# Weights turned by transposing DMAs, and a new order of the last three attention batches

## The chip, the cores and the metric

The kernel runs on one core of one Trainium2 chip. The time is device microseconds of that core for one execution; the figure given is the median of 3 runs.

## The reference

A gated block of two layers over `x` of 8 batches x 256 positions x 256 channels, all in float32. The first is single-head attention with a context of the same shape (the softmax runs over the queries of each key, axis 1), the second a gated feed-forward layer with 704 hidden units, whose inputs and weights are rounded to integers of 8 bits with a scale (per row for weights, one scale of the whole tensor for activations).

```python
def attention(q, c, Wq, Wk, Wv):
    qh, kh, vh = q @ Wq.T, c @ Wk.T, c @ Wv.T
    s = qh @ kh.T / sqrt(256)
    s = where(causal, s, -inf)
    return softmax(s, axis=1) @ vh

def ffn(x, clip_x, clip_down, w_gate, w_up, w_down):
    xq = fake_quant(x, clip_x)               # one scale: sigmoid(clip) * max|x| / 127
    gate, up = xq @ q8(w_gate).T, xq @ q8(w_up).T
    h = fake_quant(silu(gate) * up, clip_down)
    return h @ q8(w_down).T

x = x + tanh(g_xattn) * attention(layernorm(x), ctx, Wq, Wk, Wv)
x = x + tanh(g_ffn) * ffn(layernorm(x), ...)
```

The two maxima over the whole tensor (of the normalised input, and of the hidden values) are barriers: nothing behind one can start before everything ahead of it is done.

## The kernel before

All is held in SBUF. Every engine runs a program written by hand, and semaphores join them; nothing but that written order sets what an engine does next. PE is TensorE, DVE VectorE, ACT ScalarE, POOL GpSimd, SP the engine that issues most transfers.

Stage one, attention, goes over 8 batches (LAST is 7). For batch b PE makes `scores(b)` (L497), the projected queries of the next batch, `project_queries(b + 1)` (L479), the values of the batch after that, `values(b + 2)` (L457), and the weighted sum `attend(b)` (L507 to L509). DVE takes the row maxima (`row_max`, L941), ACT the exponentials (L744, L749), DVE the inverse sums, and scales the queries of the next batch by their row's inverse deviation (`scale_queries_whole`, L933, into `uT`); ACT scales the values (`values_out`, L759, into `vh`). `scores(b + 1)` waits for that `uT`. The deviations come for batches 4 to 7 by two small transfers on SP's queue (`spread`, then `r_wide`). After `attend(b)` DVE adds the residual (L955), takes the statistics for the second layer norm (L961, L967), POOL normalises (L388, into `xn2`), and DVE takes the largest absolute value (`largest2`, L972). Of the last batch the residual is made in PSUM by PE (L598 to L608), one tile in bank RB and one in SC, and DVE takes its statistics there (L1074, L1076).

The weights of the second layer are rounded meanwhile: gate and up by ACT (`quantise_weights`, the last step L773, into `wgu_q`, 6 slots of 128 rows), down by ACT and POOL (`quantise_down_weights` L778, and L404, into `wd_q`). PE needs them turned, with the contracted index on the partitions. PE turns gate and up with 24 transposes in three groups of 8 (`turn_gate_up`, L527), one group between `attend(5)` and `scores(6)` and two between `project_queries(7)` and `scores(7)`; ACT (L783, twice) and DVE (L1058) copy the results from PSUM. The down weights are turned at the end of stage two (`turn_down`, L537) and copied by ACT (L788 to L796).

The first barrier: DVE's maxima of the last two batches (L1079), then their largest (L1083), a spreading matmul on PE (L544), the scale and its inverse (L1089, L1092), then the rounded input `xq`. Stage two makes gate and up (L650) for five blocks of 128 hidden units in two halves, and a block of 64 (L669). The second barrier is the maximum of the hidden values (L1129), again through L544, L1089 and L1092. Ahead of it PE turns the residual stream (L680), which ACT copies to `x1T` (L801): six of eight copies ahead of the barrier, two behind. Stage three goes over 8 steps of 256 rows (c = 0 to 7): ACT rounds (L890), DVE clips to `hq` (L1164), PE multiplies by the down weights (L705, L710), DVE adds the residual (`finish`, L1169), SP stores.

## Time and profile before

| what | value |
|---|---|
| median of 3 runs | 109.54 us (109.43 to 109.54) |
| the profiled execution | 109.32 us, of which the trace's span is 107.4 us |
| granted clock of TensorE | full (1.00) all through |
| busy: PE, DVE, ACT, POOL | 93%, 76%, 65%, 41% of the span |
| chain that ended last, by engine | PE 52%, ACT 18%, DVE 17%, issue 4%, DMA 4% |

The chain that ended last is followed back from the last instruction, at each step to what released it. A share of it says where time was spent with nothing beside it to hide it; a busy share says only how much an engine worked.

### The profile page before, as it was taken

What the parts mean: (1) busy time and instruction counts of PE and PEld (TensorE: products, weight loads), DVE (VectorE), ACT (ScalarE), POOL (GpSimd) and SP (SyncE); (2) the same over time, 40 slices, a digit from 0 to 9 for tenths busy, and PEclk for the clock granted to TensorE, in tenths of its full rate; (3) what the DMA queues carried; (4) which work ended last, traced back from release to release, by engine and by line L of the source; (5) the groups of instructions that cost most, each with busy time, mean ns of one, the idle gap of its engine ahead of it and who ended that gap; (6) DMA issues with size and microseconds to landing.
All of it is one profiled execution on the core that took longest, in us unless ns stands there. A gap on an engine that the chain in (4) does not pass through costs nothing.

```text
span 107.4 us, 1812 instructions
## 1 busy us (share of the span) xinstructions
PE 99.9 (93%) x600; PEld 76.8 (71%) x600; DVE 81.6 (76%) x212; ACT 69.6 (65%) x131; POOL 44.2 (41%) x80
## 2 busy tenths in 40 slices
PE   5989999999999999999999987999999699999960
PEld 2268888988989897988988973444433398788850
DVE  0275296597899979868678978649999997869990
ACT  0422252567882817457677978889988899999800
POOL 7215035065371817343192593065578540520000
PEclk9999999999999999999999999999999999999999
DMA  3999999999001411305000000000000000005547
GB/s 28 383 384 260 386 419 422 410 406 395 31 23 26 33 16 14 38 1 57 0 0 0 0 0 0 6 0 3 0 0 0 0 6 0 0 0 195 195 148 249
DMA packets 5769, 12.18 MB, mean 113 GB/s; under 512 B 1280, under 2 KB 2048, under 8 KB 5760
## 3 DMA queue, kind: packets, MB, share of 16 engines
q1 hardware_dynamic: 5184, 11.28, 31.8%
q10 hardware_dynamic: 576, 0.79, 2.1%
q8 instruction: 5, 0.08, 0.3%
q14 instruction: 4, 0.03, 0.1%
HBM read 9.96 MB, written 2.10 MB: 112 GB/s over the span
## 4 chain that ended last, share of the span: by engine, by line
PE 52%; ACT 18%; DVE 17%; issue 4%; DMA 4%; ACTq 1%; DVEq 0%
PE ps L457 13%; PE ps L479 11%; PE ps L497 10%; ACT ints L890 7%; DVE shared L1124 5%; DVE hmax L1129 4%; ACT xn L801 4%; DMA wq_sb<-in_wq 4%; PE ps L650 3%; PE ps L507 3%; PE ps L509 2%; PE ps L508 2%; PE ps L554 2%; ACT silu L863 2%; PE ps L669 2%
## 5 line engine op out<-in xcount | busy, mean ns | idle before, releaser
L650 PE MATMUL ps<-xq,wguT 128*128 128x512 bf16 x80 | 17.7, 379 | 0.8 <-DVE xq L1104 0.8
L428 POOL TENSOR_TENSOR shared<-up_sb,silu 128x1024 f32<-128x1024 f32 x5 | 11.8, 2365 | 9.7 <-ACT up_sb L868 9.7
L650 PEld LDWEIGHTS ps<-xq,wguT 128*128 128x128 bf16 x80 | 7.6, 98 | 10.6 <-DVE shared L1124 1.1
L457 PE MATMUL ps<-wvT,shared 128*128 128x256 f32 x56 | 13.3, 380 | 0.0
L479 PE MATMUL ps<-shared,a_sb 128*128 128x256 f32 x56 | 13.2, 379 | 0.0
L1129 DVE TENSOR_REDUCE hmax<-shared 128x1 f32<-128x2048 f32 (+1 forms) x6 | 12.7, 2108 | 0.6
L863 ACT ACTIVATE silu<-ps,gu_scale 128x1024 f32<-128x1024 f32 x10 | 11.1, 1115 | 2.5 <-PE ps L650 2.5
L744 ACT ACTIVATE probs<-neg_scores,neg_max 128x256 f32<-128x256 f32 x8 | 4.1, 508 | 12.7 <-DVE neg_max L941 12.5
L497 PE MATMUL ps<-uT,shared 128*128 128x256 f32 (+1 forms) x64 | 11.9, 329 | 0.0
L457 PEld LDWEIGHTS ps<-wvT,shared 128*128 128x128 f32 x56 | 10.6, 190 | 1.6 <-issue 0.2
L497 PEld LDWEIGHTS ps<-uT,shared 128*128 128x128 f32 x64 | 10.7, 190 | 1.2
L705 PE MATMUL ps<-hq,wdT 128*128 128x256 bf16 x80 | 10.9, 274 | 0.3 <-DVE hq L1164 0.2
L479 PEld LDWEIGHTS ps<-shared,a_sb 128*128 128x128 f32 x56 | 10.1, 190 | 1.1
L375 POOL TENSOR_SCALAR var<-mv 128x2 f32<-128x2 f32 x8 | 1.5, 193 | 21.9 <-DVE mv L967 21.7
L890 ACT ACTIVATE ints<-shared,act_inv 128x1408 int16<-128x1408 f32 (+2 forms) x9 | 9.5, 1128 | 0.0
L759 ACT ACTIVATE vh<-ps,inv_sum 128x256 f32<-128x256 f32 x16 | 6.7, 471 | 2.8 <-DVE inv_sum L950 2.8
L1124 DVE SCALAR_TENSOR_TENSOR shared<-ps,gu_scale,silu 128x1024 f32<-128x1024 f32 x5 | 6.4, 1279 | 2.7 <-ACT silu L863 2.7
L955 DVE SCALAR_TENSOR_TENSOR xs<-ps,tanh_g,xs 128x512 f32<-128x512 f32 x7 | 5.2, 747 | 3.7 <-PE ps L509 3.7
L705 PEld LDWEIGHTS ps<-hq,wdT 128*128 128x128 bf16 x80 | 6.8, 98 | 1.5 <-DVE hq L1164 0.6
L941 DVE CUSTOM_DVE_ANT_0 neg_scores<-ps,causal 128x256 f32<-128x256 f32 (+1 forms) x16 | 5.0, 350 | 2.6 <-PE ps L497 2.6
L388 POOL TENSOR_SCALAR xn<-xs,neg_mean,rstd 128x256 f32<-128x256 f32 x12 | 6.6, 557 | 0.8 <-POOL neg_mean L383 0.2
L1169 DVE SCALAR_TENSOR_TENSOR xn<-ps,out_scale,xn 128x256 f32<-128x256 f32 x16 | 6.8, 475 | 0.0
(131 smaller groups left out, 200.0 us busy)
## 6 DMA issues: line engine op xcount, KB each, us to landing
shared<-in_xc SPq DMA_DIRECT2D x6, 512.0 KB, 10.6
out<-xn SPq DMA_DIRECT2D x7, 256.0 KB, 2.0
xs<-in_x SPq DMA_DIRECT2D x3, 512.0 KB, 8.3
shared<-in_wgu SPq DMA_DIRECT2D x3, 512.0 KB, 7.7
shared<-in_xc SPq DMA_DIRECT2D x4, 256.0 KB, 6.0
wd<-in_wd SPq DMA_DIRECT2D x1, 768.0 KB, 10.2
r_wide<-spread SPq DMA_DIRECT2D x4, 128.0 KB, 4.0
wq_sb<-in_wq ACTq DMA_DIRECT2D x1, 256.0 KB, 3.9
```

What stands on the lines that cost most here:

```text
L428: nc.gpsimd.tensor_tensor(hid[:, 2 * i + 1, :], up_sb[i % 2][:], silu1[i % 2][:], ALU.mult).then_inc(hid_done[1], 1)
L457: last = nc.tensor.matmul(bank2(VB[b])[:, k, :], ctxT(b)[:, e, k * P:(k + 1) * P], weights[:, e, :], start=(e == 0), stop=(e == KT - 1))
L479: last = nc.tensor.matmul(query_bank(b, f), a_sb[:, e, f * P:(f + 1) * P], xT(b)[:, e, :], start=(e == 0), stop=(e == KT - 1))
L497: last = nc.tensor.matmul(bank(SC)[:, c0:c0 + n], ctxT(b)[:, f, k * P:(k + 1) * P], uT[b % 2][:, f, k * P:S], start=(f == 0), stop=(f == K ...
L650: last = nc.tensor.matmul(bank(4 * half + 2 * g + c), wguT[:, i, g, k, :], xq[:, k, col:col + CH], start=(k == 0), stop=(k == KT - 1))
L705: nc.tensor.matmul(down_half(c, t), wdT[:, i, cols], hq[c % HQ_BUFS][:, 2 * i:2 * i + 2, :].rearrange("p h n -> p (h n)"), start=(i == 0), ...
L759: last = nc.scalar.activation(vh[b % 2][:, k, :], bank2(VB[b])[:, k, :], ACT.Copy, scale=inv_sum[:, b, k:k + 1])
L863: nc.scalar.activation(dst[:], ps[:, 4 * half:4 * half + 2, :].rearrange("p c n -> p (c n)"), ACT.Silu, scale=gu_scale[:, i, 0:1]).then_in ...
L890: nc.scalar.activation(hq_i16[c % HQ_BUFS][:, s0:s1, :], hid[:, s0:s1, c * P:(c + 1) * P], ACT.Copy, scale=act_inv[:, 1:2]).then_inc(hq_in ...
L1124: nc.vector.scalar_tensor_tensor(out=hid[:, 2 * i, :], in0=ps[:, 2:4, :].rearrange("p c n -> p (c n)"), scalar=gu_scale[:, i, 1:2], in1=si ...
L1129: nc.vector.tensor_reduce(hmax[:, n:n + 1], hid[:, first:first + count, :].rearrange("p s n -> p (s n)"), AX.X, ALU.max, apply_absolute_va ...
L1169: return nc.vector.scalar_tensor_tensor(out=x1T[:, c, t, :], in0=down_half(c, t), scalar=out_scale[:, t:t + 1], in1=x1T[:, c, t, :], op0=A ...
```

## The change

Three things are changed. (1) Gate, up and down weights are turned by transposing DMAs on SP's queue, from SBUF to SBUF (2 bytes an element): six of 128 x 512 for gate and up, two of 128 x 896 for down, issued behind the last `r_wide`. The transposes on PE and the copies out of PSUM go away. The down weights are laid out in 7 blocks of 128 in place of 6 (the half block stands twice, beside zeros), so its load, its rounding and its cast are 896 columns wide in place of 768. POOL's cast to `wd_q` comes ahead of the second normalisation of batch 5. (2) In the last three batches `scores(6)` and `scores(7)` come ahead of `attend(5)` and `attend(6)` in turn; half of `values(7)` is made behind them; DVE's maxima `largest2(3)` to `largest2(5)` move. (3) All eight copies to `x1T` stand ahead of the second barrier.

```diff
@@ SP
+            for s in range(SLOTS):
+                sp.wait_ge(wgu_q_done, s + 1)
+                sp.dma_start_transpose(wguT[:, s].rearrange("p n k i -> p (n k) i"),
+                                       wgu_q[:, s].rearrange("p n d -> p (n d)")).then_inc(wguT_here, 16)
+            sp.wait_ge(wd_q_done, 1)
+            for t in range(KT):
+                sp.dma_start_transpose(wdT[:, :, t * P:(t + 1) * P], wd_q[:, t]).then_inc(wdT_here, 16)
@@ POOL
+                if b == LAST - 1:
+                    pool.wait_ge(wdint_done, KT)
+                    nc.gpsimd.tensor_copy(wd_q[:], wd_i16[:]).then_inc(wd_q_done, 1)
                 if 1 <= b < LAST:
                     inverse_deviation2(b - 1)
                     apply2(b - 1)
-                if b == LAST - 1:
-                    pool.wait_ge(wdint_done, KT)
-                    nc.gpsimd.tensor_copy(wd_q[:], wd_i16[:]).then_inc(wd_q_done, 1)
@@ PE
-                values(b + 2)
+                if b + 2 < LAST:
+                    values(b + 2)
+                else:
...
+                    values_tile(LAST, 0)
                 if b + 2 < WIDE_FROM:
                     spread_deviation(b + 2)
-                attend(b)
+                if b < LAST - 2:
+                    attend(b)
 
             p = LAST % 2
-            pe.wait_ge(vh_ready, LAST - 1)
-            turn_gate_up(0, WT)
             scores(LAST - 1)
             project_queries(LAST)
-            pe.wait_ge(wguT_ready, 1)
-            turn_gate_up(1, WT)
-            turn_gate_up(2, X2)
+            attend(LAST - 2)
             scores(LAST)
             attend(LAST - 1)
-            pe.wait_ge(wguT_ready, 2)
-            transposes2(LAST - 2)
+            values_tile(LAST, 1).then_inc(v_done, 1)
...
-            for b in (0, 1, 2):
+            for b in (0, 1, 2, 4, 5):
                 transposes2(b)
-            pe.wait_ge(wguT_last, 1)
-            transposes2(4)
...
-            pe.wait_ge(wguT_ready, 2)
-            pe.wait_ge(wguT_last, 1)
+            pe.wait_ge(wguT_here, 16 * SLOTS)
...
-            pe.wait_ge(silu_done[1], FULL)
-            turn_down(0, 4)
-            turn_down(1, 5)
...
+            pe.wait_ge(wdT_here, 16 * KT)
@@ ACT
-            wguT_out(0, WT)
             exponentials(LAST - 1)
             values_out(LAST - 1)
-            wguT_out(1, WT)
...
-            wdT_out()
-            for c in range(STEPS - 2):
+            for c in range(STEPS):
                 x1T_out(c)
...
-            for c in (STEPS - 2, STEPS - 1):
-                x1T_out(c)
@@ DVE
+            row_max(LAST - 1)
+            largest2(LAST - 4)
+            invert_sum(LAST - 1)
+            scale_queries_whole(LAST)
+            largest2(LAST - 3)
+            residual(LAST - 2)
+            stats2(LAST - 2)
             row_max(LAST)
-            largest2(LAST - 2)
+            variance2(LAST - 2)
             for k in range(QT):
...
             residual(LAST - 1)
             stats2(LAST - 1)
             variance2(LAST - 1)
+            largest2(LAST - 2)
```

On PE, from the values of the last batch (the `wvT_g` rows) to the last scores (`uT1` the second time): `vh1` belongs to batch 5, `uT0` to batch 6. Before:

```order
L457 MATMUL ps<-wvT_g,shared 128x256 x4
L507 MATMUL ps<-vh1,probs0_1 128x256
L508 MATMUL ps<-vh1,probs0_1 128x256
L509 MATMUL ps<-vh1,probs1_1 128x256
L527 MATMUL ps<-ident_bf,wgu_q 128x128 x8
L497 MATMUL ps<-uT0,shared 128x256 x2
L497 MATMUL ps<-uT0,shared 128x128 x2
L479 MATMUL ps<-shared,a_sb 128x256 x4
L527 MATMUL ps<-ident_bf,wgu_q 128x128 x16
L497 MATMUL ps<-uT1,shared 128x256 x2
L497 MATMUL ps<-uT1,shared 128x128 x2
```

In the changed program, to the weighted sum of batch 6 (`vh0`), whose last two rows and the other half of the values follow:

```order
L460 MATMUL ps<-wvT_g,shared 128x256 x2
L498 MATMUL ps<-uT0,shared 128x256 x2
L498 MATMUL ps<-uT0,shared 128x128 x2
L480 MATMUL ps<-shared,a_sb 128x256 x4
L508 MATMUL ps<-vh1,probs0_1 128x256
L509 MATMUL ps<-vh1,probs0_1 128x256
L510 MATMUL ps<-vh1,probs1_1 128x256
L498 MATMUL ps<-uT1,shared 128x256 x2
L498 MATMUL ps<-uT1,shared 128x128 x2
L508 MATMUL ps<-vh0,probs0_0 128x256
```

The rows L527 are gone, two of the four value products have left the stretch, and the weighted sum of batch 5 stands behind the scores of batch 6 and the queries of batch 7.

On DVE, from the scaled queries of batch 7 (`uT1`, the last `r_wide` row) to the maxima of the last batch in PSUM. Before:

```order
L933 TENSOR_TENSOR uT1<-ps,r_wide 128x512
L1058 COPY wguT<-ps 128x1024
L972 TENSOR_REDUCE xmax<-xn2 128x1
L941 ISA neg_scores1,neg_max<-ps,causal 128x256
L941 ISA neg_max 128x1
L941 ISA neg_scores1,neg_max<-ps,causal 128x128
L941 ISA neg_max 128x1
L972 TENSOR_REDUCE xmax<-xn2 128x1
L1067 RECIPROCAL inv_sum<-row_sum 128x1 x2
L955 SCALAR_TENSOR_TENSOR xs<-ps,tanh_g,xs 128x512
L961 BN_STATS bn2<-xs 128x6 x2
L967 BN_AGGR mv2<-bn2 128x2 x2
```

In the changed program:

```order
L887 TENSOR_TENSOR uT1<-ps,r_wide 128x512
L926 TENSOR_REDUCE xmax<-xn2 128x1
L909 SCALAR_TENSOR_TENSOR xs<-ps,tanh_g,xs 128x512
L915 BN_STATS bn2<-xs 128x6 x2
L895 ISA neg_scores1,neg_max<-ps,causal 128x256
L895 ISA neg_max 128x1
L895 ISA neg_scores1,neg_max<-ps,causal 128x128
L895 ISA neg_max 128x1
L921 BN_AGGR mv2<-bn2 128x2 x2
L1023 RECIPROCAL inv_sum<-row_sum 128x1 x2
L909 SCALAR_TENSOR_TENSOR xs<-ps,tanh_g,xs 128x512
L915 BN_STATS bn2<-xs 128x6 x2
```

The copy L1058 is gone, the residual and the statistics of batch 5 now stand between the queries of batch 7 and the last row maxima, and `largest2(5)` (the second xmax row before) has left its place behind the last row maxima. It now stands behind the statistics of batch 6, ahead of those of batch 7, where the changed program goes on:

```order
L921 BN_AGGR mv2<-bn2 128x2 x2
L926 TENSOR_REDUCE xmax<-xn2 128x1
L1031 BN_STATS bn2<-ps 128x6
L1033 BN_AGGR mv2<-bn2 128x2
L1031 BN_STATS bn2<-ps 128x6
```

So the one maximum, which had the wait for the exponentials to fill, now has a place in the row of work that ends in the barrier's maximum.

On SP's queue, from the last two small transfers of the deviations to the stores, in the changed program:

```order
L330 DMA spread<-rstd1 128x2
L333 DMA r_wide<-spread 128x256
L337 DMA_TRANSPOSE wguT<-wgu_q 128x4x128 x6
L341 DMA_TRANSPOSE wdT<-wd_q 128x7x128 x2
L345 DMA out_0<-xn2 128x512 x7
L348 DMA out_0<-xn2 128x256 x2
```

The eight transposing transfers stand between the last `r_wide` and the first store; before, the stores followed at once.

## Rows read from the trace of the kernel before

**Rows 1.** Chain of waits, last three batches: start us, length us, what.

```profile
44.41 1.31 PE ps L497 x8
45.72 1.73 PE ps L479 x8
47.45 1.73 PE ps L457 x8
49.17 0.43 PE ps L507 x2
...
50.47 0.45 PE ps L527 x8
...
54.01 0.89 PE ps L527 x16
...
56.48 0.42 DVE neg_scores L941
...
58.13 0.66 DVE xs L955
...
61.02 1.29 DVE xmax L1079 x4
...
65.61 2.77 PE ps L650 x12
```

**Rows 2.** Timeline of DVE: start us, length us, engine line op.

```profile
44.45 0.75 DVE L955 SCALAR_TENSOR_TENSOR xs<-ps,tanh_g,xs 128x512 f32<-128x512 f32 x1 [0.23 <-PE ps L509]
45.23 0.75 DVE L961 BATCH_NORM_STATS2 bn<-xs 128x6 f32<-128x256 f32 x2
45.90 0.41 DVE L941 CUSTOM_DVE_ANT_0 neg_scores<-ps,causal 128x256 f32<-128x256 f32 x1
...
47.69 0.69 DVE L933 TENSOR_TENSOR uT<-ps,r_wide 128x512 f32<-128x512 f32 x1
...
57.04 0.68 DVE L972 TENSOR_REDUCE xmax<-xn 128x1 f32<-128x512 f32 x1
```

**Rows 3.** Timeline of ACT, same columns.

```profile
48.58 1.75 ACT L778 ACTIVATE wd_i<-wd,wdinv 128x768 int16<-128x768 f32 x2
...
57.89 0.84 ACT L759 ACTIVATE vh<-ps,inv_sum 128x256 f32<-128x256 f32 x2
...
60.94 0.82 ACT L841 ACTIVATE neg_dev<-ps,mv 128x256 f32<-128x256 f32 x2
```

**Rows 4.** Timeline of POOL, same columns.

```profile
53.21 0.19 POOL L375 TENSOR_SCALAR var<-mv 128x2 f32<-128x2 f32 x1 [3.83 <-DVE mv L967]
...
55.62 1.46 POOL L404 CAST wd_q<-wd_i 128x1536 bf16<-128x1536 int16 x1
```

**Rows 5.** Timeline of SP's queue, same columns.

```profile
46.88 0.32 SPq L337 DMA_DIRECT2D r_wide<-spread  x1
```

**Rows 6.** DMA issues on the page: KB each, median us to landing.

```profile
out<-xn SPq DMA_DIRECT2D x7, 256.0 KB, 2.0
...
r_wide<-spread SPq DMA_DIRECT2D x4, 128.0 KB, 4.0
```

**Rows 7.** Instructions of tile wgu_q: ns min/median/max, first and last start.

```profile
L773 ACT CAST wgu_q<-wgu_i x6: 617/618/619, 19.7 to 43.6; 128x512 bf16<-128x512 int16 x6
```

**Rows 8.** Chain of waits, after the last hidden block.

```profile
88.53 3.03 ACT xn L801 x6
...
94.47 0.95 ACT xn L801 x2
```

**Rows 9.** Timeline of DVE in the last stage.

```profile
91.48 0.87 DVE L1160 TENSOR_SCALAR ints<-shared,act_inv 128x384 int16<-128x384 f32 x2
...
96.39 0.53 DVE L1164 TENSOR_SCALAR hq<-ints 128x1408 bf16<-128x1408 int16 x1 [0.49 <-ACT ints L890]
96.84 0.87 DVE L1169 SCALAR_TENSOR_TENSOR xn<-ps,out_scale,xn 128x256 f32<-128x256 f32 x2
...
101.83 0.53 DVE L1164 TENSOR_SCALAR hq<-ints 128x1408 bf16<-128x1408 int16 x1
```

More of the change, by code:

```diff
@@ L34 @@
 SLOTS = FULL + 1
+WD_BLOCKS = FULL + 2
 STEPS = NT // 2
@@ L518, in transposes2 @@
                 last.then_inc(tr2_done, 1)
-            def turn_gate_up(n, bk):
-                pe.wait_ge(wgu_q_done, 2 * n + 2)
-                view = ps[:, bk, :].bitcast(BF16).rearrange("p (s n k i) -> p s n k i", s=2, n=2, k=KT)
-                for s in range(2):
-                    for g in range(2):
-                        for k in range(KT):
-                            last = nc.tensor.transpose(view[:, s, g, k, :],
-                                                       wgu_q[:, 2 * n + s, g, k * P:(k + 1) * P], ident_bf[:])
-                last.then_inc(wgu_tr, 1)
-            def turn_down(n, bk):
-                pe.wait_ge(wd_q_done, 1)
-                view = ps[:, bk, :].bitcast(BF16)[:, 0:3 * D].rearrange("p (s h) -> p s h", s=3)
-                for s in range(3):
-                    i0 = (3 * n + s) * P
-                    for t in range(KT):
-                        last = nc.tensor.transpose(view[:, s, t * P:(t + 1) * P], wd_q[:, t, i0:i0 + P], ident_bf[:])
-                last.then_inc(wd_tr, 1)
             def spread_max(n, bk):
@@ L682, in turn_x1 @@
                 last.then_inc(x1_turned, 1)
[L684 removed]
+            pe.wait_ge(silu_done[1], FULL)
             turn_x1(0)
             turn_x1(1)
[L687 removed]
+            pe.wait_ge(up_out_done, FULL)
             turn_x1(2)
             turn_x1(3)
[L690 removed]
+            pe.wait_ge(silu_done[0], FULL + 2)
             turn_x1(4)
             turn_x1(5)
[L693 removed]
+            pe.wait_ge(hid_done[0], FULL + 2)
             turn_x1(6)
             turn_x1(7)
[L696 removed]
+            pe.wait_ge(x1T_ready, 4)
             spread_max(1, 7)
@@ L710, in down_products @@
                             last = nc.tensor.matmul(down_half(c, t)[:, half * P:(half + 1) * P],
-                                                    wdT_rest[:, half, cols], hq[c % HQ_BUFS][:, 2 * FULL, :],
+                                                    wdT[:, FULL + half, cols], hq[c % HQ_BUFS][:, 2 * FULL, :],
                                                     start=False, stop=(half == 1))
                         last.then_inc(down_done, 1)
+            pe.wait_ge(wdT_here, 16 * KT)
             first = FIRST_SLOTS // 2
@@ L779, in quantise_down_weights @@
                     wdint_done, 1)
-            def wguT_out(n, bk):
-                act.wait_ge(wgu_tr, n + 1)
-                nc.scalar.copy(wguT[:, 2 * n:2 * n + 2].rearrange("p s n k i -> p (s n k i)"),
-                               ps[:, bk, :].bitcast(BF16)).then_inc(wguT_ready, 1)
-            def wdT_out():
-                act.wait_ge(wd_tr, 1)
-                nc.scalar.copy(wdT[:, 0:3, :].rearrange("p s h -> p (s h)"),
-                               ps[:, 4, :].bitcast(BF16)[:, 0:3 * D]).then_inc(wdT_ready, 1)
-                act.wait_ge(wd_tr, 2)
-                nc.scalar.copy(wdT[:, 3:5, :].rearrange("p s h -> p (s h)"),
-                               ps[:, 5, :].bitcast(BF16)[:, 0:2 * D]).then_inc(wdT_ready, 1)
-                act.wait_ge(rest_zeroed, 1)
-                for half in range(2):
-                    rows = slice(half * REST, (half + 1) * REST)
-                    nc.scalar.copy(wdT_rest[rows, half, :],
-                                   ps[rows, 5, :].bitcast(BF16)[:, 2 * D:3 * D]).then_inc(wdT_ready, 1)
             def x1T_out(c):
@@ L1027, in _ @@
             dve.wait_ge(consts, 3)
-            for b in range(LAST):
+            for b in range(LAST - 1):
                 if b >= 1:
@@ L1225 @@
     down = given["L0_ffn_w_down"].reshape(KT, P, I).transpose(1, 0, 2)
+    none = np.zeros((P, KT, P - REST), np.float32)
     scalars = np.concatenate([given[name].reshape(1) for name in
@@ L1235 @@
         "wgu": np.stack([slots(given["L0_ffn_w_gate"]), slots(given["L0_ffn_w_up"])], axis=2),
-        "wd": np.concatenate([down, down[:, :, FULL * P:I]], axis=2),
+        "wd": np.concatenate([down, none, none, down[:, :, FULL * P:I]], axis=2),
     }
```

45 lines of the change are left out of this document (15 added, 30 removed).

## The prediction

> **What bounds the kernel now.** I read first the page (granted clock, shares by engine, the chain by line), then the chain of waits in order of time over the last three attention batches, then the timelines of DVE, ACT, POOL and SP's queue beside it, and the chain again behind the last hidden block. The clock is full all through, so nothing hangs on it. Up to the last scores the chain is PE alone, piece behind piece: scores 1.31 us, queries 1.73, values 1.73, the three parts of a weighted sum 0.43 each [rows 1]. What PE does there ahead of the last scores is paid for in full, the turning of the gate and up weights too: 0.45 us ahead of the scores of batch 6, 0.89 ahead of those of batch 7 [rows 1]. At 56.48 DVE takes over with the last row maxima, and but for the exponentials the chain stays on DVE through the residual of batch 6 (58.13) and the four maxima (61.02) up to the barrier; PE starts stage two at 65.61 [rows 1]. Behind the second barrier ACT leads: its copies to x1T run from 88.53 to 91.56, and two more hold it for 0.95 us at 94.47 [rows 8].
>
> **The change, part by part.**
>
> *PE up to the last scores.* Same work up to the queries of batch 6, which end at 47.45 [rows 1]. Then half of the values (0.86) leads to 48.31. The scores of batch 6 wait for their scaled queries, which DVE has at 47.69 + 0.69 = 48.38 [rows 2]: call it 48.40, a new wait of 0.1. Behind the waiting PE instruction stands everything that follows, so its end counts. Then scores 1.31, queries 1.73, weighted sum of batch 5 1.30, scores of batch 7 1.31: 54.05 [rows 1], with a tail of 0.16 of the last product about 54.2, an estimate from the 45.90 at which DVE follows a product piece that ends at 45.72 [rows 1, 2].
>
> Does the second scaling hold this up? From the row maxima of batch 5 (45.90) to the end of the scaling that follows (48.38) is 2.48 [rows 2]. Those of batch 6 start at 49.9 (48.40 + 1.31 and the tail), so the scaling ends at 52.4, ahead of the 52.74 at which PE comes to the last scores. ACT must be free for the exponentials in between, 0.7 behind the row maxima, at 50.6. Its two roundings of the down weights run from 48.58 for 1.75 [rows 3]; with 896 columns for 768 I add 0.2 (a sixth of 1.75 would be 0.3, an upper bound), which gives 50.5. It just fits. The two copies of turned weights on ACT and the one on DVE go; they lay beside other work, so they are worth nothing by themselves.
>
> *DVE from there to the barrier.* DVE ends the scaling at 52.4 (the next piece can start at 52.3), takes a maximum of an already normalised batch (0.60, by 0.68 less its overlap [rows 2]) and starts the residual of batch 5 at 52.93, when PE's weighted sum is there too. From a residual to the row maxima behind it is 45.90 - 44.45 = 1.45 [rows 2], so the last row maxima start at 54.38, 0.2 behind what PE alone would allow. Before it was 56.48 [rows 1]: 2.10 us earlier. From here DVE's row is the same as before, with one piece more on it: the maximum of batch 5, which before stood at 57.04 in the hole that the exponentials leave [rows 2], now stands behind the statistics of batch 6, at 0.60. So the barrier comes 2.10 - 0.60 = 1.50 us earlier.
>
> Three others must follow. POOL normalises batch 5 from 53.21 to 55.62 [rows 4], 2.4 us behind the variance; that now comes at about 55.2, so the input of the moved maximum is there at 57.7, and DVE comes to it at 54.38 + 3.37 = 57.75 (3.37 is what lay between 56.48 and the end of the variance of batch 6, 1.7 behind 58.13 [rows 1]). That is a margin of nothing, and each tenth by which POOL is later counts. The cast of the down weights, 1.46 at 55.62 [rows 4], 1.7 with 1792 columns, goes first on POOL, from 50.5 to 52.3, so it holds up nothing, and frees POOL behind. ACT: values_out of the last batch started at 57.89 [rows 3]; it now waits for the other half of the values, 54.05 + 1.30 + 0.86 + tail = 56.4, also 1.5 earlier, so its deviations, done at 60.94 + 0.82 = 61.76 before [rows 3], are there at 60.3, and DVE's fourth maximum starts at 60.5. PE has the transposes of batches 4 and 5 behind the last products; five batches, each about a piece of 0.43 [rows 1], end at 60.6, before the spreading matmul is due at 61.3.
>
> *The transposing DMAs.* The trace has none. The last weights are rounded at 43.6 + 0.6 = 44.2 [rows 7], but SP issues the last r_wide at 46.88 for 0.32 [rows 5], and the transposes stand behind it: from 47.2. PE needs all six at 65.61 - 1.50 = 64.1. So six transfers of 128 KB have 16.9 us, 2.8 each if they don't overlap at all. Below, the cost is nothing (they overlap, and beside them the DMA engines have nothing but r_wide). Above, the slowest transfer of 128 KB in this trace, r_wide with 4.0 us to landing, six times in a row [rows 6]: 24 us, to 71.2, 7.1 late. The stores move 256 KB in 2.0 us [rows 6]; six in a row would end at 59.2. I take the lower end, hidden: contiguous rows of 1 KB read from SBUF are nearer to a store than to a broadcast of one row of HBM, and queued transfers overlap. The two down transposes can follow from 52.3 and have until 91 even at 4.0 each. SP's stores come behind them at 95, so its queue is free.
>
> The Trainium skill has a rule that speaks against this. "VectorE: DVE Perf Modes", section "The three transpose paths", puts one 128 x 128 block of 2 bytes at 1309 ns by DMA and 390 ns on TensorE; here a group of 8 blocks took PE 0.45 us, 56 ns each in the row [rows 1], so the page's figure for TensorE does not hold for blocks in a row. If the page's DMA figure held in a row for 24 blocks, it would be 31.4 us, to 78.6, 14.5 us late, and the time some 122 us; no run yet shows it.
>
> *Loads.* The down weights' load is 896 KB for 768, and the cover is that its first reader, and those of the loads behind it, come microseconds after the last load. Nothing counted.
>
> *Behind the second barrier.* ACT's eight copies to x1T, 3.03 / 6 = 0.51 each, take 4.0 us from about 86.7 and end before the barrier. ACT then starts rounding with DVE, at 91.48 in place of 91.56 [rows 8, 9]: 0.08. The 0.95 of copies leaves ACT's row [rows 8]. But the pitch of stage three was (101.83 - 96.39) / 4 = 1.36, and DVE alone needs 0.45 for a clip (96.84 - 96.39) and 0.87 for two finishes [rows 9], 1.32 and small gaps. So little of the 0.95 comes through: over some five steps 0 to 0.2. With the 0.08 I take 0.15 in all; bounds 0 and 0.95 + 0.08.
>
> **Sum.** 109.32 - 1.50 - 0.15 = 107.67 for a profiled execution; the median of the runs is 0.22 above the profiled one, so 107.9.
>
> **The rivals.**
> 1. *The transposes are late* (slower). PE's first gate product waits for the sixth. It costs nothing up to 16.9 us for the six and decides the sign at 18.5 us, 3.1 each in a row. With 4.0 each: 109.54 - 1.65 + 7.1 = 115.0. For it: a 2-byte transpose writes pieces much smaller than a store's; against it: 17 us with idle DMA engines. 0.15. The rule above is this case at its worst.
> 2. *The transposes push back the last r_wide* (slower). DVE now wants it at 49.9 + (47.69 - 45.90) = 51.7 [rows 2]; it lands at about 46.88 + 4.0 = 50.9 [rows 5, 6], a margin of 0.8. Its data shares the DMA engines with transposes issued right behind it. If landing takes 8.0 for 4.0, the scaling starts 3.2 late, and the time is 107.9 + 3.2 = 111.1; the sign turns at 2.4 us of delay. Against it: it was issued first on the same queue. 0.06.
> 3. *The front gives less.* DVE has almost no slack in the new order: the late normalisation by POOL, ACT's rounding, the residual ahead of the row maxima each can add some tenths. Gain 0.3 to 1.1, time 108.4 to 109.2. 0.12.
> 4. *Nothing comes of it*: 109.3 to 109.8, if two of those meet. 0.05.
> The forecast has 0.62, with a range of its own of 107.4 to 108.4 (front 1.1 to 1.7, end 0 to 0.5).
>
> **How the numbers follow.** 0.2% is 0.22 us, about what a measurement of this kernel can tell. Faster: 0.62 + 0.12 = 0.74; same 0.05; slower 0.15 + 0.06 = 0.21. The range reaches from 107.3 (a bit more of the 0.95 comes through) over rivals 3 and 4 to 109.8, and leaves out the two slower cases.
>
> **What would show it.** In the changed profile: scores of batch 6 near 48.4 with a wait of about 0.1 for the scaling; the last row maxima at 54.4; the first maximum over the deviations at 59.5; the first gate product at 64.1, released by DVE's xq. If it is released by a DMA, rival 1; if the scaling of batch 7 waits for a DMA, rival 2; if largest2(5) waits for POOL, rival 3. Landing times of the transposes: under 2.8 each in a row. Stage three's pitch 1.33 to 1.36, released by DVE or PE and no more by ACT. What would make it wrong is above all a transposing DMA of several microseconds.

## The result, and the profile after

The changed kernel takes **106.86 us** (median of 4 runs, 106.51 to 106.93) beside 109.54 of the kernel before on the same chip: ratio 0.9749, 95% interval 0.9726 to 0.9772, 2.7 us less. The forecast was 107.9 us with a range from 107.3 to 109.8. The sign came as said, by the front part that was named, but the time lies below the range. The comparison was made twice more, on other occasions, each time with its own runs of before: 0.9805 (0.9773 to 0.9838) and 0.9822 (0.9789 to 0.9856), 2.0 to 2.1 us less. So the gain is 2.0 to 2.7 us, and why it varies is a question of its own below. A ratio leaves out executions in a slower state of the chip, which shows as a lower granted clock or as a time over 1.5% above the kernel's fastest.

The page of the changed kernel: span, busy time by engine, the granted clock and DMA rows in 40 slices, and the chain by engine.

```profile
span 104.7 us, 1734 instructions
PE 97.4 (93%) x562; PEld 75.0 (72%) x564; DVE 80.7 (77%) x211; ACT 66.1 (63%) x125; POOL 43.9 (42%) x79
PEclk9999999999999999999999999999999999999999
DMA  3999999999323010402946500000000000005555
DMA packets 10888, 13.54 MB, mean 129 GB/s; under 512 B 6400, under 2 KB 7168, under 8 KB 10880
PE 56%; DVE 28%; ACT 6%; issue 4%; POOL 3%; DVEq 0%; POOLq 0%
```

ACT's share of the chain fell from 18% to 6%, and the page's summary of the chain lists no DMA. The transposes are the 9465 in the middle of the DMA row (50 to 60 us); no engine waits for them. The chain of waits from batch 6 to the first gate product, against [rows 1]:

```profile
48.35 1.59 PE ps L498 x8
...
56.08 0.66 DVE xs L909
...
59.58 1.29 DVE xmax L1036 x4
```

The timeline of DVE in the same stretch (start us, length us), against [rows 2]:

```profile
47.61 0.69 DVE L887 TENSOR_TENSOR uT<-ps,r_wide 128x512 f32<-128x512 f32 x1
...
51.77 0.69 DVE L887 TENSOR_TENSOR uT<-ps,r_wide 128x512 f32<-128x512 f32 x1
...
54.45 0.41 DVE L895 CUSTOM_DVE_ANT_0 neg_scores<-ps,causal 128x256 f32<-128x256 f32 x1
...
57.81 0.69 DVE L926 TENSOR_REDUCE xmax<-xn 128x1 f32<-128x512 f32 x1
```

Then those of ACT, POOL and SP's queue, against [rows 3 to 5]:

```profile
48.49 1.97 ACT L755 ACTIVATE wd_i<-wd,wdinv 128x896 int16<-128x896 f32 x2
```

```profile
50.52 1.68 POOL L404 CAST wd_q<-wd_i 128x1792 bf16<-128x1792 int16 x1 [1.38 <-ACT wd_i L755]
```

```profile
47.22 0.32 SPq L333 DMA_DIRECT2D r_wide<-spread  x1
47.58 7.82 SPq L337 DMA_TRANSPOSE wguT<-wgu_q  x6
55.45 2.64 SPq L341 DMA_TRANSPOSE wdT<-wd_q  x2
```

The last row maxima start at 54.45 and not at 56.48, the first maximum over the deviations at 59.58 and not at 61.02 in the chain. Six transposes are issued in 7.82 us, one each 1.30; in the third comparison's profile the six took 9.95. On the page their landing stands beside that of the loads and stores, against [rows 6]:

```profile
out<-xn SPq DMA_DIRECT2D x7, 256.0 KB, 2.0
...
r_wide<-spread SPq DMA_DIRECT2D x4, 128.0 KB, 3.9
...
wguT<-wgu_q SPq DMA_TRANSPOSE x6, 2.5
wdT<-wd_q SPq DMA_TRANSPOSE x2, 3.0
```

The last of the six is issued at 54.1 and is there at about 56.6, 7.5 us before the first gate product is due (the page has 78 of the 80 gate and up records of L630, so the first shown, at 64.38, may not be the first made). In the last stage, ACT and then DVE, against [rows 8, 9]:

```profile
89.71 9.36 ACT L846 ACTIVATE ints<-shared,act_inv 128x384 int16<-128x384 f32 x9 [0.75 <-DVE act_inv L1049]
```

```profile
92.79 0.56 DVE L1121 TENSOR_SCALAR hq<-ints 128x1408 bf16<-128x1408 int16 x1 [0.37 <-ACT ints L846]
...
94.05 0.51 DVE L1121 TENSOR_SCALAR hq<-ints 128x1408 bf16<-128x1408 int16 x1
...
95.27 0.51 DVE L1121 TENSOR_SCALAR hq<-ints 128x1408 bf16<-128x1408 int16 x1
...
99.11 0.53 DVE L1121 TENSOR_SCALAR hq<-ints 128x1408 bf16<-128x1408 int16 x1
...
100.58 1.80 DVE L1126 SCALAR_TENSOR_TENSOR xn<-ps,out_scale,xn 128x256 f32<-128x256 f32 x4 [0.17 <-PE ps L686]
```

Two more lines of before belong beside these, a clip ahead of those in [rows 9] and the finishes at the end:

```profile
94.56 0.57 DVE L1164 TENSOR_SCALAR hq<-ints 128x1408 bf16<-128x1408 int16 x1 [0.36 <-ACT ints L890]
...
102.27 2.44 DVE L1169 SCALAR_TENSOR_TENSOR xn<-ps,out_scale,xn 128x256 f32<-128x256 f32 x6
```

Before, the clips stood 1.83 us apart once (94.56 to 96.39, with ACT's two copies in between), then four times 1.36, 7.27 in all. Changed, the same five distances are 1.26, twice 1.22, 1.26 and at last 1.36 again, 6.32 in all (92.79 to 99.11). The last clip comes 0.95 us earlier, the whole length of the two copies. ACT itself still needs 1.36 for a step of 1408 columns, as two more lines of its timeline show (starts of pieces), and PE, on which the chain stays to the end, 0.66 for half a step:

```profile
94.90 2.81 ACT L846 ACTIVATE ints<-shared,act_inv 128x1408 int16<-128x1408 f32 x2
96.26 2.81 ACT L846 ACTIVATE ints<-shared,act_inv 128x1408 int16<-128x1408 f32 x2
```

```profile
96.60 0.55 PE ps L681 x5
97.14 0.11 PE ps L686 x2
97.25 0.55 PE ps L681 x5
```

With the two spans cut at four marks, the 2.7 us fall into pieces (the spans are printed to 0.1 us, so the last piece is no more exact):

| stretch | before | after | difference |
|---|---|---|---|
| start to the first stage-two rounding on DVE (63.85, 62.41) | 63.85 | 62.41 | -1.44 |
| from there to the last stage's first rounding (91.48, 89.71) | 27.63 | 27.30 | -0.33 |
| from there to the end of DVE's last finish (104.71, 102.38) | 13.23 | 12.67 | -0.56 |
| from there to the end of the span | 2.7 | 2.3 | -0.4 |

The experiments ask what makes each of these, and what makes the runs of the changed kernel differ. Unless said otherwise each starts from the changed kernel. A ratio is to the kernel before, run beside the variant; its median was 109.5 to 109.6 each time.

### The profile page after: what moved, and what is told of

It is laid out like the page before. It is cut to its first block, busy times and chain, and to the rows that moved or that the text cites. A ratio compares the mean times of both kernels' runs of the same rounds, so it can differ in the third digit from the quotient of the medians.

```text
span 104.7 us, 1734 instructions
## 1 busy us (share of the span) xinstructions
PE 97.4 (93%) x562; PEld 75.0 (72%) x564; DVE 80.7 (77%) x211; ACT 66.1 (63%) x125; POOL 43.9 (42%) x79
## 3 DMA queue, kind: packets, MB, share of 16 engines
q1 hardware_dynamic: 10304, 12.66, 37.8%
## 4 chain that ended last, share of the span: by engine, by line
PE 56%; DVE 28%; ACT 6%; issue 4%; POOL 3%; DVEq 0%; POOLq 0%
PE ps L460 12%; DVE hmax L1086 9%; PE ps L681 9%; PE ps L480 8%; PE ps L498 8%; PE ps L450 4%; DVE shared L1081 4%; PE ps L630 2%; POOL shared L431 2%; PE ps L508 2%; DVE bn L915 2%; PE ps L510 2%; PE ps L509 2%; DVE xs L909 2%; PE ps L535 2%
## 5 line engine op out<-in xcount | busy, mean ns | idle before, releaser
L630 PE MATMUL ps<-xq,wguT 128*128 128x512 bf16 x78 | 17.2, 379 | 1.1 <-DVE xq L1061 1.0
L630 PEld LDWEIGHTS ps<-xq,wguT 128*128 128x128 bf16 x80 | 7.8, 98 | 10.2 <-issue 1.0
```

The source lines that it names most:

```text
L630: last = nc.tensor.matmul(bank(4 * half + 2 * g + c), wguT[:, i, g, k, :], xq[:, k, col:col + CH], start=(k == 0), stop=(k == KT - 1))
```

## Experiments

**The last stage: ACT's two late copies.** First they go back behind the barrier, with all else as changed:

```
-            for c in range(STEPS):
+            for c in range(STEPS - 2):
                 x1T_out(c)
...
             hidden_ints(2, 0, THIRD_ACT_SLOTS)
+            for c in (STEPS - 2, STEPS - 1):
+                x1T_out(c)
```

> The changed kernel with the last two copies to x1T back behind the second barrier, where the kernel before had them: 0.95 us more on ACT ahead of its rounding of step 3. The prediction's theory (DVE's own pitch of 1.32 us bounds stage three, so the copies are worth 0.1 or so): 107.0 us. The theory from the trace after (ACT's late rounding made DVE do its last six finishing pieces in one burst behind the last clip, and the last three stores in one burst behind them): all that stage three and its tail gained, up to 0.9 us, comes back: 107.6 to 107.8 us, with DVE's last piece again some 0.9 us behind PE's last product in place of 0.6.

Beside it the changed kernel itself:

> The changed kernel itself, as a base for the others of this call. 106.9 us (106.7 to 107.1). The open question is the gap of 0.4 us on DVE ahead of the second product of stage two, there in the trace of the kernel before and not in that of the changed one: if it belongs to the program, it is absent here too; if it comes and goes, it may be here.

Measured: 108.40 us (0.9888, interval 0.9853 to 0.9923) against 107.41 (0.9805). By the ratios that is 0.9 us, with 0.5 of uncertainty. DVE's timeline with the copies back:

```profile
94.85 0.53 DVE L1123 TENSOR_SCALAR hq<-ints 128x1408 bf16<-128x1408 int16 x1 [0.49 <-ACT ints L846]
...
100.73 2.44 DVE L1128 SCALAR_TENSOR_TENSOR xn<-ps,out_scale,xn 128x256 f32<-128x256 f32 x6
```

This is the picture of before: the clip waits for ACT, and six finishes are left for one burst at the end. From DVE's first rounding to its last finish it takes 13.23 us, to the hundredth what before took, and the tail 2.5 for 2.3. So in the trace the copies cost 0.56 + 0.2, about 0.7 to 0.8 us.

Then the same question asked of the kernel before (the waits for eight copies are lowered to six as well):

```
-            for c in (STEPS - 2, STEPS - 1):
-                x1T_out(c)
```

> The kernel before, with ScalarE's two copies of the last two blocks of the transposed stage-two input left out (the last steps then read stale columns there, and the output of those is another). Everything else is as before. Theory 'the two copies set the pitch of stage three': ScalarE's integers and with them VectorE's clips come 0.95 us earlier, VectorE's last six finishing pieces spread out, the last stores too: 0.6 to 0.95 us less than the kernel before, so 108.6 to 108.9 us. Rival (the prediction's own reading, TensorE's 1.32 us a step bounds): 0.15 to 0.3 us less, 109.2 to 109.4. Its VectorE instructions are those of before up to the end of stage two: if the 0.41 us ahead of product(1) belong to the kernel before, they are here again.

0.9955 (0.9926 to 0.9985), 0.5 us less, between the two theories. Its profiled execution ran with a granted clock of 0.853 throughout (span 131.1 us), so its rows don't price the copies. It was made again, with the pause of the next paragraph out of the way:

> The kernel before with the four small VectorE instructions at its start (109.11 us measured) and with ScalarE's two late copies left out (the last two blocks of the transposed stage-two input stay stale, and the output of the last steps is another). Theory 'the two copies set the pitch of stage three': 0.6 to 0.9 us less than 109.11, so 108.2 to 108.5 us, and in the profile VectorE's finishing pieces no longer end in a burst of six. Rival (TensorE's pitch bounds): 108.8 to 109.0 us.

108.79 us, 0.9938 (0.9914 to 0.9962), where its base had 0.9953 (0.9935 to 0.9972) in another comparison: 0.2 us less, with 0.3 of uncertainty, the size the rival gave. But the trace shows the mechanism at work. DVE's burst of six became one of four, and from DVE's first rounding to its last finish it took 12.66 us for 13.23. The tail gives some of it back, 2.8 us for 2.7, and the spans of the two profiles differ by 0.4. So the copies are worth 0.56 on DVE in either kernel; how much of it reaches the end of the kernel before is between nothing and 0.5.

The tail has a second cause. Two of the last stores of 256 KB landed after 3.2 and 2.9 us in this profile and after 3.3 and 2.5 in that of before, all of them after 2.0 to 2.1 in all kernels that turn the down weights by DMA, the one that turns gate and up on PE included. A fetch of 16 KB of instructions stands just there, at 101.5 here and at 102.3 in before; the DMA queues of before from 101 to 106 us have it, those of the changed kernel from its first store on have none:

```profile
q8 instruction: 1, 0.02, 1.6%
```

All four profiles of kernels made from before have five such fetches, the fifth while the last stores are under way; all 14 others have four, the last of them done before the first store is issued. No run moved the fetch alone, so the slow stores go with the fetch, and that it makes them slow is not shown.

**Stage two: a pause of 0.41 us.** In before the chain of waits has this ahead of DVE's second product (of after's it has no such line):

```profile
71.53 0.03 issue
71.56 0.02 DVEq L1123
71.58 0.41 issue
72.00 1.29 DVE shared L1124
```

The semaphore is through at 71.58, and the product starts at 72.00. By then both profiles with 4.00 us from product(0) to product(1) had product(1) at place 171 of DVE's instructions (counted from 0, as built), and all with 3.62 or 3.63 had it at 170. Four tiny instructions at the start of before move it to place 175:

```
+            for n in range(4):
+                nc.vector.memset(spot[:, n:n + 1], 0.0)
             dve.wait_ge(wq_here, 16)
```

> The kernel before with four VectorE instructions of about 0.05 us more at its very start, where VectorE waits for the first load anyway. Theory 'the 0.41 us ahead of product(1) hang on where that instruction stands in the engine's stream': the pause is gone or stands at another instruction, and the time is up to 0.35 us less. Rival 'chance of one execution': the pause shows or not with no change in the median, 109.4 to 109.7 us.

109.11 us, 0.9953 (0.9935 to 0.9972): 0.5 us faster than before (0.3 to 0.7), by four instructions more. The distance is 3.62, and stage two takes 27.30 us for 27.63. Then the other way round, one such instruction in the changed kernel, which puts product(1) from place 170 to 171:

> The changed kernel with one VectorE instruction of 0.05 us more at its very start, where the engine waits anyway. It moves product(1) from the 170th to the 171st place of VectorE's stream, where it stands in the kernel before (counted from 0, as built). Theory 'the pause hangs on the place in the stream': product(0) to product(1) grows from 3.63 to 4.00 us, and the time by 0.3 to 0.4 us over the run above. Rival 'chance, or the kernel's other state': 3.63 us, and no difference.

Its chain:

```profile
70.42 0.41 issue
70.83 1.29 DVE shared L1084
```

The pause is back, the distance is 4.00, and stage two takes 27.62 us for 27.30. Against the changed kernel run beside it,

> The changed kernel once more, beside the next three on the same chip. Theory 'thin margin': median 106.8 to 107.4 us, with runs up to 1 us above the fastest; its pauses ahead of product(1) stay away (product(0) to product(1) 3.6 us).

the time is no longer (107.14 against 107.55), where 0.3 to 0.4 more was expected: that kernel's runs were spread by something larger, below, so this pair doesn't price the pause. That the pause hangs on the place is shown by the traces: of the 16 at full clock through stage two, the three with place 171 have it and the 13 with 170 or 175 don't. Its price of 0.33 us is from the traces and from before_tiny4. Its mechanism stays open: the fetches of instructions that the DMA queues show stand at other times (67.4 and 72.6 in before, whose pause is from 71.6 to 72.0).

**The front: a scaling that waits for a small load.** The changed kernel's later comparisons were slower than the first, and its runs reach from 106.5 to 108.8. The third comparison's chain of waits says why for one of these runs (its profile is 1.1 us longer than the first; 0.3 of that stands ahead of the scaling of batch 6, 47.90 against 47.61):

```profile
48.18 4.59 DMA r_wide<-spread
...
52.89 0.69 DVE uT L887
```

The scaling of batch 7 now wants r_wide(7) at 51.8 to 52.1; before it wanted it at 54.12. From the issue of the spreading transfer (44.0 to 44.3) to the landing of r_wide(7) it took 7.1 us in the first profile and 8.5 in this one, and DVE stood 0.77. The kernel before had 3.2 us to spare in its profile, and 1.5 in the least of its variants, so the same variation didn't show. The first profile of the changed kernel had 0.7. This is rival 2's place. Is it rival 2's cause, the transposes behind it?

The earlier batches answer a part of that. A load r_wide is issued when its spreading transfer has landed, so the distance of the two issues is the landing of the small one. Batch 5, in the first profile and then in the third:

```profile
31.89 0.32 SPq L330 DMA_DIRECT2D spread<-rstd  x1
34.38 0.32 SPq L333 DMA_DIRECT2D r_wide<-spread  x1
```

```profile
32.15 0.32 SPq L330 DMA_DIRECT2D spread<-rstd  x1
35.88 0.32 SPq L333 DMA_DIRECT2D r_wide<-spread  x1
```

2.5 us and 3.7 us, some 12 us ahead of the first transpose. The profiles fall into two groups by this: in five the spreading transfers of batches 5 and 6 took 3.6 to 4.1 us, in the other 13 from 2.5 to 3.4. One of the five is a variant of before that turns everything on PE, and every profile in which DVE stood for r_wide(7) (0.77, 1.29, 0.73 and 0.21 us) is among the other four. So in some profiles the small transfers take long from early on, with or without the transposes.

Then the transposes were held back until r_wide(7) was there:

```
+            sp.wait_ge(r_wide_here[B - 1 - WIDE_FROM], 16)
             for s in range(SLOTS):
                 sp.wait_ge(wgu_q_done, s + 1)
```

> The changed kernel, with one more wait on the issuing queue: the six transposes of gate and up start only when r_wide(7) has landed (near 51.2 us instead of 47.6), so that the two never share the transfer engines. All six land by about 60.3 us instead of 56.6, still 3.8 us ahead of need. Theory 'the transposes slow the small load': r_wide(7) lands in 3 us or less each time, the runs lie close together near 106.8 us. Rival 'the load's time varies by itself': it still takes 3 to 6 us, and the runs spread by 1 to 2 us as those of the changed kernel.

106.79 us (106.72 to 107.35), 0.9753 (0.9726 to 0.9779); r_wide(7) landed in 3.4 us. That alone would speak for the transposes, but this profile is not one of those five. The other way is to send the load earlier, batch 7's statistics one batch ahead on DVE and POOL (`if b + 4 == LAST: stats1(LAST); variance1(LAST)` behind the pair of batch b + 3, and the same for POOL's inverse deviation):

> The changed kernel, with the statistics and the inverse deviation of batch 7 one batch earlier on VectorE and GpSimd, so that its spreading transfer and the load of r_wide(7) leave some 3 us earlier. Theory 'thin margin': the changed kernels differ by 1 to 2 us from run to run because r_wide(7) has about 0.6 us to spare ahead of batch 7's scaling; with 3 us more the time is 106.6 to 107.0 us in nearly every run, and no wait of VectorE's scaling for r_wide shows. Rival 'the spread is the chip's': the runs stay 1 to 2 us apart, with the first wait elsewhere (the start's loads, the last stores).

107.22 us, and the five runs within 0.5 us (107.00 to 107.53), 0.9786 (0.9760 to 0.9811). The runs lie close as expected, but not for the reason given. The spreading transfer was issued at 41.8, 2.2 us earlier, right behind r_wide(6) in the queue, and took 4.9 us; r_wide(7) was issued at 46.70 and landed at 51.5, where the first profile had it at 51.1. It had 0.7 us to spare, as there. So this base is steadier in its runs, and that the edit made it so is not shown. Both together:

> The changed kernel with both: batch 7's statistics one batch earlier, and the transposes held back until r_wide(7) has landed. Theory 'two small transfers with too little to spare': the lowest spread of all, 106.6 to 106.9 us. Rival 'what is left is the start's loads': the same 107.0 to 107.5 as with the first alone.

107.55 us (107.09 to 108.27), 0.9824 (0.9791 to 0.9857): the rival, if anything, and wider apart than with the first alone. r_wide(7) took 4.6 us with no transpose near it, and the scaling waited 0.21. Landing times of r_wide(7) over all profiles: 3.4, 4.6 with the transposes held back; 4.0 to 4.7 in the five kernels where they aren't there; 3.9 to 4.8, once 6.2, where they are right behind. So the load varies by itself, and that the transposes add to it is not shown.

**The front: what the order is worth.** With the order of before for the last three batches, and the turns still by DMA:

> The changed kernel (weights turned by DMA, copies ahead of the barrier) with the old order of the last three batches on PE and DVE. If the whole front gain is the turning that left PE (1.5 us): no change, 106.9. My theory: without the turning, PE reaches the last scores 0.8 us before their scaled queries are ready (row maxima of batch 6 at 51.9, and 2.45 us from there to the end of the scaling, so 54.35 for 53.5), so the new order is worth about 0.75 us: 107.6 (107.4 to 107.8), and a wait of PE for DVE's scaling of 0.8 us ahead of the last scores.

108.56 us, 0.9892 (0.9854 to 0.9931), beside 107.41. But r_wide(7) had landed after 6.2 us in its profile, and the scaling waited 0.73 for it. So it was done again on the steadier base (`values(b + 2)` and `attend(b)` for every b, and DVE's maxima after them):

> The same, with the last three batches in the order of before (the weights still turned by transfers). Theory: the reorder is worth what TensorE's waits for the last scaling and the last row maxima cost, some 0.7 us, so about 0.75 us longer than the run above (107.3 to 107.8). Rival: if the transfers alone removed the work that mattered, 0.2 us or less longer.

107.91 us (0.9851, 0.9826 to 0.9876) against 107.22: 0.7 us, with 0.4 of uncertainty. The timeline of PE shows what the reorder removes:

```profile
55.26 1.57 PE L500 MATMUL ps<-uT,shared 128*128 128x256 f32 x8 [0.99 <-DVE uT L882]
```

Without turns between them, the last scores come to the scaling too early and wait 1 us; the reorder fills that with a weighted sum and half of the values. And the maximum of batch 4 (LAST - 3) behind the last row maxima, where DVE has a hole:

```
-            largest2(LAST - 3)
             residual(LAST - 2)
             stats2(LAST - 2)
             row_max(LAST)
             variance2(LAST - 2)
+            largest2(LAST - 3)
```

> The changed kernel with DVE's maximum of batch 4 moved from behind the scaling of batch 7 to behind the last row maxima, where DVE waits for the exponentials. DVE is then free 0.6 us earlier, and PE's last scores (54.26) set the last row maxima in place of DVE (54.45): 0.2 us faster, 106.7. If the hole is too short for it (0.3 and 0.2 us idle around the two inverse sums), the residual of batch 6 starts later by what is lacking, up to 0.1 us, and the gain is 0.1.

107.47 us, 0.9808: no difference to its neighbour, but DVE waited 1.29 for r_wide(7) in the profile. On the steadier base:

> The kernel with batch 7's statistics one batch earlier, and the maxima of the normalised batch 5 moved on VectorE from ahead of the last row maxima to the hole behind them. VectorE idles there 0.3 to 0.5 us in the changed kernel, and the last row maxima start up to 0.6 us earlier: 0.2 us less than its base (107.2 us in its own comparison), so 106.9 to 107.1. Rival: the last row maxima wait for TensorE's scores in either place, and nothing changes.

The edit is the same one, of batch 4 and not 5. 107.17 us, 0.9775 (0.9751 to 0.9799) against 107.22: nothing, as the rival said, but by another wait. The residual of batch 5 waits 0.53 us for PE's weighted sum and starts at 53.52 (53.45 with the maximum ahead of it), and the last row maxima follow it. The barrier's first maximum stands at 60.03, where it stood (59.97). No variant was measurably faster than the first comparison of the changed kernel; the nearest, with the transposes held back, has 0.9753 beside 0.9749.

**The front: what the turns on PE cost.** Gate and up turned by PE and copied as before, in the new order:

```
+            turn_gate_up(0, WT)
             scores(LAST - 1)
             project_queries(LAST)
+            pe.wait_ge(wguT_ready, 1)
+            turn_gate_up(1, WT)
+            turn_gate_up(2, X2)
             attend(LAST - 2)
```

> The same as the first, with the gate and up weights turned on TensorE again and copied by GpSimd, VectorE and ScalarE, in the new order; the down weights stay with the transfers. Theory: the six turns of TensorE (about 0.45 us each with their waits and copies) come back onto the path of the last three batches: 1.2 to 2.0 us longer than the first run. Rival: with the scores ahead TensorE has slack for them, and it costs under 0.5 us.

(ACT and DVE copy, none of it is GpSimd's.) 109.13 us (0.9964, 0.9944 to 0.9985) against 107.22, 1.9 us. The timeline of PE has the cost, and the chain stays on it:

```profile
49.24 0.62 PE L528 MATMUL ps<-ident_bf,wgu_q 128*128 128x128 bf16 x8 [0.43 <-ACT vh L756]
49.70 1.53 PE L498 MATMUL ps<-uT,shared 128*128 128x256 f32 x8
...
52.79 1.06 PE L528 MATMUL ps<-ident_bf,wgu_q 128*128 128x128 bf16 x16
```

The scores of batch 6 start 0.9 us later than in the base (49.70 against 48.81), 0.14 of which both kernels' scaling of batch 6 already shows (48.20 against 48.06), and the other sixteen transposes add 0.89: 1.77 to the barrier's first maximum (61.74 against 59.97). The rest is the pause again, for this kernel's one DVE copy more puts product(1) at place 171 (distance 4.00).

Four profiles now have all four pairs of turning and order. From the scaling of batch 6 to the first rounding of `xq` on DVE it took:

| | order of before | new order |
|---|---|---|
| turned on PE | 16.16 (63.85 - 47.69, before) | 16.45 (64.65 - 48.20) |
| turned by DMA | 15.69 (64.14 - 48.45) | 14.82 (62.88 - 48.06) |

(All but the first have the statistics of batch 7 one batch earlier; the changed kernel itself has 14.80.) The transfers alone are worth 0.5 us, the new order alone costs 0.3, and the two together gain 1.3. In the old order the transposes on PE took time in which PE would else have stood for the last scaling, 0.99 us of it; with them gone, the new order has that to fill.

**The transposes: how near are they to being late?** All six made twice, the second six behind the landing of the first:

```
+                sp.dma_start_transpose(...).then_inc(wguT_once, 16)
+            sp.wait_ge(wguT_once, 16 * SLOTS)
+            for s in range(SLOTS):
+                sp.dma_start_transpose(...).then_inc(wguT_here, 16)
```

> The same as the first, with all six gate and up weights transposed twice by the queue: the second six start when the first six have landed. The first six land some 7.5 us before the first gate product; six more take 6 x 1.3 us and the wait for the first landing 1.2 us, so the last lands about 9 us later, near 65.7 instead of 56.6, 1.6 us after the first gate product could start at 64.1. Theory 'a queue at 1.3 us each, that delays nothing else': 1.0 to 1.8 us longer than the first run. Rival 'contention': more, with r_wide or the softmax stage later too. Rival 'the transposes run side by side': 0.3 us or less.

0.9927 (0.9892 to 0.9962) in the four runs with the clock full (108.1 to 109.3), 1.5 us over early7, in the middle of what the queue theory gave. Seven of its eleven runs were longer, 110.0 to 110.7, with a mean granted clock of 0.98, and the profile is one of these. The timelines of SP's queue and of PE, and then the windows of the stretch (busy us of PE, PEld, DVE, ACT and POOL, then PEclk, TensorE's granted clock, and the DMA share):

```profile
57.80 7.74 SPq L342 DMA_TRANSPOSE wguT<-wgu_q  x6
```

```profile
67.04 5.30 PE L637 MATMUL ps<-xq,wguT 128*128 128x512 bf16 x16 [3.00 <-DMA wguT<-wgu_q]
```

```profile
66.00:68.00 2.00, 0.96 (x5) 0.59 (x7) 0.00 (x0) 0.03 (x1) 0.00 (x0) 0.97 0.69 133
68.00:70.00 2.00, 2.00 (x6) 0.68 (x5) 0.50 (x1) 1.08 (x1) 0.00 (x0) 0.50 0.61 116
70.00:72.00 2.00, 2.00 (x8) 0.78 (x7) 1.97 (x2) 0.85 (x1) 0.00 (x0) 0.68 0.04 8
```

The second set is issued in 7.74 us again, and the last lands at 66.8. PE starts 2.2 us later than early7's 64.85. Then, behind 3.0 us of standing, the granted clock falls to 0.50, the lower of its two levels (1.2 GHz of 2.4), from 67.9 to 71.3, and DVE's second product comes 3.74 us late where the first was 2.47 late: 1.3 us more, from a wait that is long over. In most runs a late transpose costs more than its lateness.

## Why the prediction was wrong, step by step

- **PE up to the last scores: right.** Scores of batch 6 at 48.35 behind DVE's scaling, 48.40 said; ACT free for the exponentials (50.46 against 50.5); scaling of batch 7 at 51.77 (51.7).
- **DVE to the barrier: right.** Row maxima at 54.45 (54.38), the moved maximum at 57.81 (57.75), the first maximum over the deviations 1.44 us earlier (1.50), and the first rounding by as much. Both parts of the change are needed for it: turns back on PE cost some 1.6 us net of the pause, the old order 0.7, and the new order without the transfers would have been a loss of 0.3.
- **The transposes: right, with more room than said.** 1.30 us each in the queue, 2.5 to landing, hidden by 7.5 us. The rule of the Trainium skill ("VectorE: DVE Perf Modes", section "The three transpose paths") of 1309 ns for a block of 128 x 128 doesn't hold here for blocks in a row: one transfer of four such blocks takes that long in the queue, 0.33 us a block, and one of seven blocks 1.34.
- **The step that failed** is the one behind the second barrier: "But the pitch of stage three was (101.83 - 96.39) / 4 = 1.36, and DVE alone needs 0.45 for a clip (96.84 - 96.39) and 0.87 for two finishes [rows 9], 1.32 and small gaps. So little of the 0.95 comes through: over some five steps 0 to 0.2." With the 0.08 it took 0.15; measured are 0.56 in DVE's row and about 0.2 in the tail. The pitch was counted from behind the wait that the copies made: from 94.56 to 96.39 the clips stood 1.83 apart, 1.26 in the changed kernel, so 0.57 comes from that one gap and would have come with a pitch of 1.32 too. [rows 9] had the wait, 0.49 at 96.39, and the prediction kept the 0.95 only as its bound. The other 0.38 lies in the four steps of 1.36: that is ACT's pitch, and DVE, with ACT's results ready ahead of it, clips every 1.22 until it has caught up, since pieces that don't wait for anybody overlap by some 0.07. The sum of DVE's durations was taken as its bound, from a stretch in which DVE waited for ACT. What did bound, and was in no term, is PE: of the 0.95 that the last clip gained, 0.39 is lost again by the last finish (3.27 us behind the last clip, 2.88 before), with PE at 1.31 a step.
- **Stage two** has no term in the sum. It gave 0.33 us, a pause of the kernel before that the change removed by moving DVE's instructions by one place. The prediction read the chain of before but not this 0.41 of "issue" in it.
- **The tail** has none either. It gave 0.4: 0.1 to 0.2 from the copies, the rest where the slow last stores of before stand beside a fetch of instructions, which no experiment tried apart.
- **How the misses add up.** Forecast for a profiled execution 107.67, measured 106.51: of the 1.16 between them 0.4 is the last stage, 0.4 the tail and 0.3 the pause; the front gave 0.06 less than said. The range reached 0.6 below the forecast, so none of the three alone would have left it. It was the mechanism of the last stage that was wrong; the other two were not looked at.
- **Rival 2** was given 0.06 and its place is real: in one profile of three of the changed kernel DVE stood 0.77 us for r_wide(7), and up to 1.29 in a variant. Its cause, the transposes behind the load, is not shown; small transfers that take long stand ahead of them in the same profiles. At this price the sign never hung on it. Sum of the pieces: 1.44 + 0.33 + 0.56 + 0.4 = 2.7; less 0.77 of waiting it is 1.9, near the 2.0 of the third comparison, whose profile has that wait. The second comparison gained 2.1, and its one profile, of its fastest execution, has no such wait, so for it this is not shown.

## What to carry to other kernels

When two engines pass work down a line, a pitch counted from behind a wait leaves out what the wait cost. The sum of an engine's durations isn't its pitch either, and a stretch paced by another engine doesn't show it: ask who is waited for there, how far its queue is ahead, and take a delay of that engine's start as fully on the path until the line shows stock. A change that tightens a schedule also spends the margin of small transfers: list those that land within 1 us of their reader, for these vary by more than that. Two parts of a change can each be worth little or less than nothing alone: measure all four pairs. And before a gain of 0.3% is explained by an edit, see whether an instruction moved by one place alone does it.

## Unexpected of the hardware

- One instruction's place in DVE's stream costs 0.38 us: product(0) to product(1) took 4.00 us in every profile with the second at place 171 and a full clock, 3.62 or 3.63 at 170 and 175. Four useless instructions made the kernel before 0.5 us faster (0.3 to 0.7).
- A load of 128 KB spread from one row took between 3.4 and 6.2 us to land, at the same place of nearly the same program; a transfer of 1 KB ahead of it 2.5 to 4.5, and 4.7 to 5.8 where it was issued right behind another such load. Long landings come together: in five profiles of 18 the small transfers of two batches on end took 3.6 to 4.1, in the others 2.5 to 3.4.
- Of the last stores of 256 KB one landed after 3.2 or 3.3 us and the next after 2.5 to 2.9 in the kernels that turn the down weights on PE, whose fifth fetch of 16 KB of instructions stands beside them (2.4 and 2.7 in the profile at a lower clock); all after 2.0 to 2.1 in those that turn them by DMA and have four such fetches. Whether the fetch does it is open.
- A transposing DMA of 128 x 512 held the queue 1.30 us and one of 128 x 896 1.34: nearly the same for four blocks and for seven.
- After 3.0 us of waiting PE's granted clock went to 0.50 for 3.4 us, from 0.8 us after PE had taken up work again.
